# Linear layer: the normalisation of x two batches ahead waits for GpSimd's addition of the output bias row

## The reference

```python
x = x + _L0_attn_ref(_layernorm(x), qkv, proj)            # causal attention, 16 heads, 4 key/value heads
x = x + _L0_ffn_ref(_layernorm(x), weight, bias, ...)     # a second layer norm, ternary weights
x = x + _L1_attn_ref(_layernorm(x), W_in, b_in, W_out, b_out)   # linear attention
x = x + _L1_ffn_ref(_layernorm(x), gate, up, down, ...)   # gated layer
```

```python
def _L1_attn_ref(X, W_in, b_in, W_out, b_out):
    QKV = jnp.einsum('bsd,ed->bse', X, W_in) + b_in
    Q, K, V = jnp.split(QKV, 3, axis=-1)
    Q = rope(Q, rot_dim)
    K = rope(K, rot_dim)
    A = jnp.sum(feature_map(K) * V, axis=-2)      # one vector per batch
    Y = A[:, None, :] * Q
    Y = jnp.einsum('bsd,ed->bse', Y, W_out) + b_out
    return Y + X
```

## Time and profile before

| | us |
|---|---|
| median of three timed runs | 578.76 |
| lowest and highest of them | 578.47, 580.87 |
| the profiled execution's own time | 580.42 |
| its span in the profile | 578.6 |
| TensorE busy in the span | 562.7 (97%) |
| VectorE busy | 469.3 (81%) |
| ScalarE busy | 370.7 (64%) |
| GpSimd busy | 220.5 (38%) |

### The profile page before, as it was taken

The page is one execution under the profiler, slowest core; times in us unless marked ns, Lnnn a source line. Parts: engine busy times, 40 slices in busy tenths (PEclk is TensorE's granted clock), DMA queues, the critical chain, the costliest instruction groups (busy, mean ns, idle before and its releaser), DMA issues.

```text
span 578.6 us, 12867 instructions
## 1 busy us (share of the span) xinstructions
PE 562.7 (97%) x4131; PEld 530.6 (92%) x4131; DVE 469.3 (81%) x1475; ACT 370.7 (64%) x1037; POOL 220.5 (38%) x324
## 2 busy tenths in 40 slices
PE   8999999999999999999999999999998999999995
PEld 7899999999999999999999999999998888778884
DVE  5888789778877987897789779977887999778875
ACT  5987566657655666575567657557876777454452
POOL 4782224233322522342232233323457678503320
PEclk9999999999999999999999999999999999999999
DMA  8806000000000000000000000000000000001011
GB/s 330 289 1 228 2 2 2 1 1 0 0 0 0 0 0 0 0 0 0 0 0 0 0 0 0 0 0 1 1 1 2 0 2 1 2 0 37 23 33 57
DMA packets 9152, 14.71 MB, mean 25 GB/s; under 512 B 1568, under 2 KB 6688, under 8 KB 9120
## 3 DMA queue, kind: packets, MB, share of 16 engines
q1 hardware_dynamic: 9120, 14.30, 7.0%
HBM read 12.20 MB, written 2.10 MB: 25 GB/s over the span
## 4 chain that ended last, share of the span: by engine, by line
PE 80%; DVE 10%; ACT 5%; issue 3%; POOL 1%; DMA 0%; DVEq 0%; SPq 0%; POOLq 0%
PE bank L651 65%; PE bank L737 5%; PE bank L753 4%; PE bank L756 2%; PE bank L661 2%; ACT prob L1143 1%; PE bank L866 1%; DVE raw L1787 1%; DVE xn_b L1754 1%; DVE prob L1552 1%; DVE qkv L1767 1%; ACT raw L1339 1%; DVE pT L1498 1%; ACT big L1116 0%; DVE oT L1498 0%
## 5 line engine op out<-in xcount | busy, mean ns | idle before, releaser
L526 POOL TENSOR_SCALAR prob<-prob,rowinv 128x256 f32<-128x256 f32 (+1 forms) x127 | 96.3, 770 | 266.1 <-DVE rowinv L1568 266.1
L651 PE MATMUL bank<-xT,big 128*128 128x256 f32 x984 | 129.7, 284 | 0.1
L651 PEld LDWEIGHTS bank<-xT,big 128*128 128x128 f32 x984 | 123.4, 192 | 1.0 <-issue 0.3
L1143 ACT ACTIVATE prob<-prob,negmax 128x128 f32<-128x128 f32 (+1 forms) x256 | 112.8, 445 | 8.3 <-DVE negmax L1552 8.3
L651 PE MATMUL bank<-wp,oT 128*128 128x256 f32 x768 | 102.5, 283 | 0.3 <-DVE oT L1498 0.3
L651 PEld LDWEIGHTS bank<-wp,oT 128*128 128x128 f32 x768 | 96.8, 190 | 1.1 <-DVE oT L1498 0.5
L1105 ACT ACTIVATE qT<-bank 128x512 fp32r<-128x512 f32 x68 | 40.6, 597 | 72.1 <-PE bank L651 72.0
L651 PE MATMUL bank<-pT,v 128*128 128x512 f32 (+1 forms) x384 | 79.8, 343 | 1.2 <-DVE pT L1498 1.2
L651 PEld LDWEIGHTS bank<-pT,v 128*128 128x128 f32 x384 | 63.2, 189 | 10.2 <-issue 1.4
L1498 DVE TENSOR_TENSOR pT<-bank,pT 128x512 fp32r<-128x512 f32 (+1 forms) x128 | 65.2, 551 | 2.9 <-ACT pT L1105 2.9
L1105 ACT ACTIVATE pT<-bank 128x512 fp32r<-128x512 f32 (+1 forms) x128 | 55.2, 484 | 12.1 <-PE bank L753 10.0
(11 more groups left out here) (186 smaller groups left out, 962.2 us busy)
## 6 DMA issues: line engine op xcount, KB each, us to landing
raw<-in_wq SPq DMA_DIRECT2D x4, 512.0 KB, 7.1
raw<-in_wp SPq DMA_DIRECT2D x4, 512.0 KB, 7.5
x<-in_x SPq DMA_DIRECT2D x7, 256.0 KB, 7.2
out<-x SPq DMA_DIRECT2D x7, 256.0 KB, 2.1
raw<-in_w_gu SPq DMA_DIRECT2D x2, 640.0 KB, 5.0
raw<-in_w_in SPq DMA_DIRECT2D x1, 768.0 KB, 4.7
raw<-in_w_down SPq DMA_DIRECT2D x1, 640.0 KB, 6.7
raw<-in_wk SPq DMA_DIRECT2D x1, 512.0 KB, 4.0
```

Source lines behind the costliest of these rows:

```text
L526: m = pool.tensor_scalar(prob[:, j % 2, 0, a:b], prob[:, j % 2, 0, a:b], rowinv[:, j % 2, r:r + 1], None, ALU.mult)
L651: m = pe.matmul(out, lhs(a), rhs(b), start=first and i == 0, stop=last and i == len(passes) - 1, skip_group_check=True)
L1143: m = act.activation(prob[:, j % 2, i, a:b], prob[:, j % 2, i, a:b], ACT.Exp, scale=-1.0, bias=negmax[:, 2 * i + r:2 * i + r + 1], accum_o ...
```

## The change

VectorE waits at the top of its `linear(n)`, for n of 2 and more, until GpSimd has added the output bias row of batch n - 2. In iteration n the semaphore has to reach n - 1, which is the count that `add_bank(n - 2)` waits for later in the same iteration. Nothing else is changed; the instructions of all engines and their order are the same. Lines behind the insertion have numbers one higher in the changed kernel.

```diff
@@ -1801,6 +1801,7 @@
 
             def linear(n):
                 if n > 1:
+                    dve.wait_ge(s_lres, n - 1)
                     linear_apply(n + 1) if n + 1 < NB else gated_apply(0)
                     q_products(n - 1)
                     if n == 2:
```

## The result

The changed kernel takes 583.55 us (median of 7 runs, 582.20 to 583.90), the kernel before 580.36 us in 7 runs that include the three shown ahead. The ratio is 1.0056, with a 95% interval from 1.0043 to 1.0069: 3.2 us slower.

A forecast was written before the change was run, and what follows sets the result against it. Took TensorE, nearly full but waiting each batch for VectorE's `k_copy` chain, as the linear layer's bound. Terms 2.2 + 0.3 + 0 + 0.3 + 0.3 + 0.2 = 3.3 us on 578.76 gave 582.1 us, range 580.4 to 583.3.

The forecast's parts named there:

- the first rival: Linear layer: only the stall at n = 2 counts, the small terms come to nothing; 581.0 us, chance 0.27.
- What bounds the layer: Linear layer: TensorE nearly full but waiting for VectorE each batch, 0.33 us before batch 3's products; later `k_copy` delays TensorE equally.
- the first stall: VectorE's apply at n = 2 waits for GpSimd's power and then bias addition after the ternary variance: +2.2 us.
- The rival of the hidden stall: Linear layer: TensorE's own work bounds the iteration, so 2.2 us melts to about 0.8; 579.6 us, chance 0.08.
- n = 2: Apply in iteration 2 starts late, behind GpSimd's power and addition: +2.2 us, bounds 1.7 and 2.3.
- n = 3: Apply in iteration 3: both tiles now come behind GpSimd's second addition: +0.3 us, bounds 0 and 0.4.
- n = 4: Apply in iteration 4: addition ends 0.75 us before the apply starts, so the wait is covered: 0 us.
- n = 5: Apply in iteration 5 starts after the addition instead of running beside it: +0.3 us, bounds 0.2 and 0.5.
- n = 6: Apply in iteration 6: both tiles come behind GpSimd's gated-weights piece following the addition: +0.3 us, bounds 0 and 0.4.
- n = 7: Apply in iteration 7 waits briefly, then starts together with GpSimd's power: +0.2 us, bounds 0.1 and 0.9.
- The power as a neighbour: GpSimd's power holds up the apply at n = 7, or a neighbour does so elsewhere: 582.8 us, chance 0.13.
- The other side: Linear layer: the wait parts applies from GpSimd's work at n = 3, 5, 6, saving 3.4 us; 577.6 us, chance 0.04.

The follow-up runs named there:

- One column of the bias row: Kernel before, with GpSimd's linear_bias adding one of the 256 bias columns, the other 255 left out: 577.03 us, ratio 0.9941.
- the reversed kernel: Kernel before, with GpSimd's bias addition waiting for VectorE's apply beside it (iterations 1 to 6), VectorE waiting for nothing new: 578.66 us, ratio 0.9978.
- both reversed kernels: The reversed kernel, and the same with the addition of iteration 4 waiting for nothing new: 577.51 us, ratio 0.9947 to the kernel before.

## Why the prediction was right or wrong

**The step that failed is the base.** The text made the sum against the profiled execution first, "that execution's own time, 580.42 us, about 583.7"; measured were 583.67 in the profile and 583.55 as the median. It then took the forecast "against the median", 578.76 us, a median of three of which two were of the rare short kind. The median of 7 executions was 580.36 us, 1.60 above that base; of all 61 it is 580.3. The other term was 0.1 too high, 3.2 us for 3.3, and 1.6 less 0.1 is the 1.5 us by which the forecast missed. From 580.36 the same terms give 583.7 us. The range had no term for this, though the profiled execution 1.7 us above the median, and the third run 2.1 us above it, said that the base was that unsure. That two of three executions were of the kind of which 11 in 61 are was bad luck; that the text trusted three was not. It also took half a per cent for about what a measurement of this kernel can tell; the intervals here reach 0.10 to 0.15% to either side. (The lower end of the range, the first rival less 0.5, comes to 580.5 and not 580.4.)

**What bounds the layer: right.** `k_copy` and the k products behind it moved by the whole of the first stall, and TensorE's 1.26 us of idle time (1.2 foretold) and 1.05 more ahead of the products (as much again) came where they were foretold. The rival of the hidden stall is refuted by this and by the wait at n = 2 alone.

**The terms.** n = 2: 2.2 foretold, 2.13 measured; the power did become 0.13 us shorter (0.70 for 0.83 us), as the lower of the two starts had it, and the signal back took 0.03 us. n = 3: 0.3 and 0.25. n = 4: 0 and 0. n = 5: 0.3 and 0.32. n = 6: 0.3 and 0.24. n = 7: 0.2 and 0.09. The sum was 3.3 and is 3.0, and 0.2 us of the difference of the spans lie ahead of the layer.

**The power as a neighbour.** The apply of n = 7 ran from 493.85 for 0.73 us with this power beside it:

```profile
493.92 0.70 POOL L455 TENSOR_TENSOR ternary_rstd<-ternary_variance,exponent 128x2 f32<-128x2 f32 x1
```

Both took their ordinary time, so the bound of 0.9 and the 582.8 us that went with it are out. The Trainium skill's exclusive lock, in "SBUF — State Buffer", section "Who interferes with whom", would have made one of the two wait for the other; for a power of 128x2 elements the trace again does not show it. In the kernel before, a power that starts 0.14 or 0.16 us behind an apply takes 0.83 or 0.80 us, so up to 0.13 us of waiting may be there, on GpSimd's side. Where the long additions are concerned the lock is seen: at n = 3 of the changed kernel the first tile of the apply ends at 462.34, 0.15 us behind GpSimd's second addition (462.19).

**The other side.** One column of the bias row saves 3.3 us, close to the 3.4 us that the rival counted, but that is luck: the parts are others. With one column the applies of n = 3 and 6 still take 1.50 us each, behind the GpSimd instruction that follows the small addition, and n = 5 takes 0.70: 1.9 us together. Another 0.66 us come from the subtraction of the down weights at n = 3 and 0.85 us from the ternary variance at n = 6, which the rival had not counted. The change could not reach any of these, for the reason given, that the wait ends no apply sooner than the addition did. That an edit of the opposite direction brings both long applies down to 0.73 us was not foreseen. The rival named the price and the text stopped at refuting it.

## What to carry to other kernels

When two engines hold each other up, a wait on the one that stands on the critical path only turns a long instruction into a wait; the wait belongs on the engine that has idle time, and there only where nothing urgent stands behind it, as iteration 4 of the reversed kernel shows. Before a wait is added, ask what the awaited instruction itself stands behind: here it stood behind a power that waited for the waiting engine's last result. And take a base time from as many executions as the answer has to be sharp: three were not enough for half a per cent.

## What the runs showed of the hardware

The 128x768 subtraction of the down weights on VectorE (line 1841) took 0.95 us with GpSimd's long additions out of the way (the one column and both reversed kernels, at n = 3), 1.61 us beside one. The ternary variance of 128x2 elements at n = 6 took 1.02 us in before and 0.17 us in the reversed kernel, so a tiny instruction pays as much as a big one when it comes up beside an addition. The other way about, GpSimd's addition of iteration 5 took 2.00 us instead of 1.28 in the changed kernel when it met the subtraction on VectorE; with one column it took 0.91 us instead of 0.19 at that place, the same 0.72 us more. Between two instructions of GpSimd back to back one VectorE tile that already waits slips through: without the waits the first of the two tiles ends 0.15 to 0.16 us behind the first addition (1.03 and 1.39 us). With the waits both tiles come behind the second instruction: the first ends at 462.34 behind 462.19 at n = 3, and at 486.15 behind 486.00 at n = 6.
